# Second cross attention of a Perceiver-like model: how many tiles TensorE takes in a row, and where its groups begin

## What is computed

```
def _L1_xattn_ref(x, context, mask, Wq, Wkv, Wout, b_out):
    q = x @ Wq.T
    k, v = jnp.split(context @ Wkv.T, 2, axis=-1)
    # 16 heads of 64; 64 queries and 1601 keys for each batch
    sim = jnp.einsum('bhid,bhjd->bhij', q, k) * SCALE
    sim = jnp.where(mask[:, None, None, :], sim, max_neg)
    attn = jax.nn.softmax(sim, axis=-1)
    out = jnp.einsum('bhij,bhjd->bhid', attn, v)
    return out @ Wout.T + b_out
```

## Time and profile before

| | us |
|---|---|
| median of three runs | 3600.09 |
| lowest and highest | 3599.73, 3602.97 |
| the profiled execution: time | 3611.44 |
| the profiled execution: span of its trace | 3609.6 |
| PE busy over the span | 3310.2 (92%) |
| mixes of this stage, first and last start | 1524.3, 3039.4 |

### The profile page before, as it was taken

One profiled execution on the slowest core, in us unless ns is written; L12 is line 12 of the kernel. 1 busy time (PEld: TensorE's weight loads), 2 busy tenths in 40 slices (PEclk: granted clock), 3 DMA queues, 4 the chain that ended last, 5 costly groups with the idle time before them and its releaser, 6 DMA issues. The chain is left out here.

```text
span 3609.6 us, 67171 instructions
## 1 busy us (share of the span) xinstructions
PE 3310.2 (92%) x26109; PEld 1922.9 (53%) x26235; DVE 2414.8 (67%) x5544; ACT 1942.3 (54%) x2669; POOL 1586.5 (44%) x1235
## 2 busy tenths in 40 slices
PE   6789999999995679599999999999999998979998
PEld 3456666666663467354555454555455554655555
DVE  6757777777774443477777777777777775563333
ACT  4446666566664322566666666666666664532222
POOL 4333333333330000277777777777777776210000
PEclk7679999999997769699999999999999998979999
DMA  1033333333320000210111111101111100010000
GB/s 56 20 70 75 75 75 79 72 74 75 83 52 1 1 24 1 70 37 20 37 37 37 37 37 37 37 22 34 37 37 37 37 28 1 1 74 1 1 1 12
DMA packets 90493, 139.18 MB, mean 39 GB/s; under 512 B 14464, under 2 KB 67776, under 8 KB 89408
## 3 DMA queue, kind: packets, MB, share of 16 engines
q1 hardware_dynamic: 90176, 134.87, 13.8%
HBM read 94.41 MB, written 1.05 MB: 26 GB/s over the span
## 5 line engine op out<-in xcount | busy, mean ns | idle before, releaser
L2120 ACT ACTIVATE arena<-banks,arena 128x512 f32<-128x512 f32 x832 | 560.9, 687 | 477.5 <-PE banks L1913 476.6
L1938 PE MATMUL banks<-arena 128*128 128x512 f32 x1664 | 804.5, 603 | 3.0 <-ACT arena L2127 3.0
L1872 POOL TENSOR_TENSOR arena<-arena 128x1024 f32<-128x1024 f32 x256 | 604.0, 2359 | 166.8 <-ACT arena L2127 165.7
L1119 DVE TENSOR_REDUCE arena<-banks 128x1 f32<-128x512 f32 (+1 forms) x896 | 529.8, 628 | 189.5 <-PE banks L1004 184.3
L2022 DVE TENSOR_TENSOR banks<-arena,banks 128x512 f32<-128x512 f32 x640 | 444.6, 695 | 242.8 <-ACT arena L2120 222.9
L1216 ACT ACTIVATE arena<-banks 128x1024 f32<-128x1024 f32 (+1 forms) x448 | 425.1, 964 | 317.0 <-PE banks L1025 314.1
L2039 DVE TENSOR_TENSOR arena<-arena,banks 128x1024 f32<-128x1024 f32 (+1 forms) x448 | 507.5, 1134 | 1.5 <-PE banks L1928 1.0
L2127 ACT ACTIVATE arena<-arena 128x1024 f32<-128x1024 f32 (+1 forms) x448 | 443.0, 989 | 11.6 <-DVE arena L2039 11.4
L1938 PEld LDWEIGHTS banks<-arena 128*128 128x128 f32 x1664 | 290.0, 190 | 223.1 <-issue 202.8
L1913 PE MATMUL banks<-arena 128*128 128x512 bf16 x831 | 314.7, 379 | 2.6
L1912 PE MATMUL banks<-arena 128*128 128x512 bf16 x785 | 298.8, 381 | 4.3 <-issue 0.2
(11 more groups left out here) (345 smaller groups left out, 5218.6 us busy)
## 6 DMA issues: line engine op xcount, KB each, us to landing
arena<-in_ctxT SPq DMA_DIRECT2D x64, 800.5 KB, 5.6
arena<-arena SPq DMA_DIRECT2D x768, 50.0 KB, 2.2
arena<-in_ctx SPq DMA_DIRECT2D x32, 768.0 KB
arena<-in_m2w SPq DMA_DIRECT2D x3, 2048.0 KB, 12.0
arena<-in_xw SPq DMA_DIRECT2D x1, 2048.0 KB, 7.4
weights<-in_weights SPq DMA_DIRECT2D x1, 1918.0 KB, 7.4
arena<-in_ctx SPq DMA_DIRECT2D x32, 32.5 KB
arena<-in_m1w SPq DMA_DIRECT2D x1, 1024.0 KB, 6.2
```

The lines of the kernel that those rows point to most:

```text
L1119: eng.tensor_reduce(o, s, AX, ALU.max).then_inc(a_max, 1)
L1872: eng.tensor_tensor(part, part, tiles, ALU.add).then_inc(sums, 1)
L1938: eng.matmul(c.ps[:, R_MIX + v % 2, :], ctxn[:, b, kt * D:(kt + 1) * D], st[:, v % 2, kt, :], start=kt == 0, stop=kt == KT - 1).then_inc(m ...
L2120: eng.activation(st[:, v % 2, kt, :], c.ps[:, n % SB, :], ACT.Identity, bias=hide[:, kt, v // 2:v // 2 + 1])\
```

## The change

TensorE's groups no longer follow the pairs of a unit. They are runs of three tiles (`SB`) counted through the whole stage, so that they go across the ends of units. Since 13 = 4 x 3 + 1, a group starts at `kt` 0 in every third unit, and the groups of the two units after it are shifted:

- unit mod 3 = 0: (0 1 2) (3 4 5) (6 7 8) (9 10 11) (12 and the next unit's 0 1)
- unit mod 3 = 1: (2 3 4) (5 6 7) (8 9 10) (11 12 and the next 0)
- unit mod 3 = 2: (1 2 3) (4 5 6) (7 8 9) (10 11 12)

Within a group the order stays: scores, small work, mixes. The orders of VectorE, ScalarE and GpSimd, and all waits, are as they were.

```diff
-        for v in range(UNITS + 1):
-            for j, a, z in tile_pairs:
-                tiles = range(v * KT + a, v * KT + z)
-                for n in tiles:
-                    if n + LEAD < TILES:
-                        scores(n + LEAD)
-                for n in tiles:
-                    between(n)
-                for n in tiles:
-                    if n < TILES:
-                        mix(n)
+        for first in range(0, TILES + KT, SB):
+            tiles = range(first, min(first + SB, TILES + KT))
+            for n in tiles:
+                if n + LEAD < TILES:
+                    scores(n + LEAD)
+            for n in tiles:
+                between(n)
+            for n in tiles:
+                if n < TILES:
+                    mix(n)
```

## The result

The changed kernel takes 3738.17 us (median of 4 runs, 3734.96 to 3742.93) beside 3601.53 for the kernel before on the same chip: 136.6 us more, a ratio of 1.038, 95% interval 1.0362 to 1.0398. Its profiled execution has a span of 3741.1 us, against 3609.6 before, 131.5 more. In what follows, "the stage" is the time from the first mix to the last (weight loads of L1938): 1524.3 to 3038.9 before, 1514.6 us.

What follows compares the result with a forecast made beforehand. TensorE was taken to bound the kernel, with nothing left over in this stage. Waits of 34 + 35.7 + 18.9 + 7.4 + 30 + 4 = 130 us took the median from 3600.1 to 3730; 8-in-10 range 3690 to 3775.

Steps and rivals of the forecast that it cites:

- The bound: TensorE, 99.57 of 100 us busy in this stage: a wait put on its path is paid in full.
- What the change takes away: TensorE turns from scores to mixes 282 times instead of 455: taken as zero, at most 3.5 us saved.
- a rival of 17: Small work comes free in time and only fewer turns are left: gain of 0 to 17 us, chance 0.04.
- (a): Projection, then transposes, groups (3 4 5): start T + 4.9 (T: first score matmul), 20 waits of 1.7, 34 us.
- (b): `spread_shift` behind the last shift: groups (6 7 8) wait 1.7, 35.7 us in all; (7 8 9) wait 0.9, 18.9.
- groups (8 9 10): `spread_shift` there: shift ends within 0.1 of TensorE's arrival; taken as nothing, 4 us as upper end.
- (c) to (e): Waits: denominators then projection, 7.4 us; queries then queries or final, 30; final then denominators, 4.
- The clock: Rival: granted clock falls with TensorE's pauses, 40 to 80 us more, 3770 to 3810, chance 0.07.
- The waits neither shrank nor grew: Two rivals: waits share causes and shrink, 3698, chance 0.08; or delayed copies make them grow, 3770, chance 0.07.

Runs made afterwards that it cites:

- Groups of one: Changed kernel with groups of one tile and VectorE's shift of the single tile at step 5 in place of step 7: 3599.4 us, ratio 0.9979.
- the change with its waits cured: Changed kernel with small work directly before its own tile's mix, and the single tile's shift at step 5: 3606.4 us, ratio 0.9998.
- the experiment that removed all but 1.4 of them: Changed kernel with VectorE's shift of the single tile at step 5 in place of step 7: 3678.2 us, ratio 1.0204 to the kernel before.

## Why the prediction was right

**The bound.** "A wait that is put on TensorE's path here is paid in full": right. New waits of 128.1 us by the rows, 131.3 us in the stage, 131.5 in the span, 137 between the medians; 130 were predicted. (The upper ends listed in the sum add up to 160.5 and not to 163; nothing hangs on it.)

**What the change takes away.** Predicted nothing, at most 3.5 us for 173 turns, with a rival of 17. Groups of one (1.50 us a tile at 390 more turns) and the change with its waits cured (ratio 0.9998) both show nothing; the bound is 0.011 us a turn, 1.9 us in all.

**(a) Projection and transposes.** Predicted 34, waits of 1.7; 35.9 shown, one of them at the stage's end, and the start at T + 4.87 where T + 4.9 was said. The size was right, the words were not quite: I put it down to a chain of maximum, shift and projection. The experiment that took the shift out of the chain moved the wait by 0.07 us. What binds is that VectorE's 1.51 us of projection steps can't begin before TensorE's projection ends; the chain ahead of it happened to end at the same moment (2228.18 against 2228.0).

**(b) `spread_shift`.** Predicted 54.6 (1.7 and 0.9, 21 times each), 54.7 shown by the rows in 42 waits, and 61.0 of time saved by the experiment that removed all but 1.4 of them. What was mis-sized is where the wait ends: I counted from T + 1.95 to the end of the shift, T + 3.66, which is where it ended; but `spread_shift` started 0.14 after that, at T + 3.80, so the wait cost 1.85 where the row says 1.69. That groups (8 9 10) cost nothing was right, since no more than 42 waits stand there.

**(c) to (e).** Predicted 7.4, 30 and 4; shown 5.8, 29.5 (22.4 and 11.3 less 4.2) and 3.8.

**What I missed.** The kernel before was not without waits in this stage, as I read from 99.57 of 100 us: 0.18 us in each unit at the transposes, 11 us in all, hidden in the weight loads' row and in the modelled ends of matmuls. The change takes it away in the units where the transposes stand a group behind the projection (2201.58 to 2201.80 in its trace, 0.22 apart): some 42 times 0.18, or 7.6 us. This gain and the 6.7 us by which (b) was too cheap nearly cancel, and the clock fell once less than in the trace before. So the sum of 130 fits better than its parts; that much of it is luck.

**The rivals.** The clock stayed at 1.00 through pauses of 1.7 us that came twice in 7 us. The first pause of the earlier trace rows had said so. But the margin was smaller than the two pauses of the earlier trace rows, 1.67 and 2.98, made it look. In the stages of the twelve kernels 266 pauses of 1.5 to 1.9 us left the clock alone, while of 21 pauses of 2.05 to 3.73 us 19 were followed by 0.50 within 3 us, those of 2.05 and 2.06 among them; the two others, of 2.34 and 2.45, are in the changed kernel. So in a kernel whose waits were like the 2.05 and 2.06 of the experiments, this rival would have been in play. The waits neither shrank nor grew when they came in every unit (1.74 us each for the transposes in both kernels, but for the ones at the stage's end). The turns were worth nothing once the pieces came free in time.

## What to carry to other kernels

Where an engine written out by hand is the bound, look for pairs of its instructions that are tied together through another engine, and count what stands between them: in this kernel a group's size mattered only through this. A longer or shifted group can bring two such pieces next to each other, and then the other engine's whole answer is idle time; the price can be read from a trace in which they are apart, by counting from the start of the group to the end of the answer. And if a bound engine seems to leave nothing, compare the distances between starts with those in a plain stream, for the busy share rounds small waits away.

## What the runs showed of the hardware

The idle time in front of a matmul is counted from the modelled end of the matmul before it, which in a stream of bf16 matmuls of 512 columns lies 0.16 us behind the next start (0.38 long, 0.22 apart). So taking away 53.3 us of shown waits, in 42 places, saved 61.0. Going between bf16 and fp32 matmuls of 512 columns cost nothing that the traces resolve: 1.50 us a tile at one turn for each tile, 3.01 us for two tiles at one turn. After pauses of 1.5 to 1.9 us, 266 of them, the granted clock never fell from 1.00 (2.4 GHz); after pauses of 2.05 us and more it fell to 0.50 (1.2 GHz) in 19 cases of 21, and three fp32 mixes then took 4.33 us in place of 2.58.
